# Twelve tiles' columns loaded from a second layout, three tiles projected by an uncentred W_in, and the first group's norm in two halves

## The reference

```python
def rmsnorm(x, g): return x * rsqrt(mean(x * x) + eps) * g
h = einsum('bld,ed->ble', rmsnorm(layernorm(x), g_res), W_in) + b_in
h_patch = rmsnorm(ctx, g_init)[..., :512]
# scan over the context rows, s[i] = a * s[i - 1] + u[i], with u and a from dt and h_patch
plug = clip(cumsum(boundary_mask) - 1, 0, 3201)     # boundaries from cumsum(mask)
x = x + s[plug] + h
x = x + gelu(layernorm(x) @ w1 + b1) @ w2 + b2      # 512 -> 2048 -> 512
```

## Time and profile before

| what | value |
|---|---|
| time, median of 3 runs | 837.85 us (837.53 to 838.92) |
| the profiled execution, its own time | 837.43 us |
| its span on the core | 835.7 us |
| PE busy | 826.4 us, 99% |
| DVE, ACT, POOL busy | 315.2, 294.5, 256.3 us |
| granted TensorE clock | 1.00 |

### The profile page before, as it was taken

The page is one execution under the profiler, slowest core; times in us unless marked ns, Lnnn a source line. Parts: engine busy times, 40 slices in busy tenths (PEclk is TensorE's granted clock), DMA queues, the critical chain, the costliest instruction groups (busy, mean ns, idle before and its releaser), DMA issues.

```text
span 835.7 us, 10792 instructions
## 1 busy us (share of the span) xinstructions
PE 826.4 (99%) x3770; PEld 680.8 (81%) x3770; DVE 315.2 (38%) x513; ACT 294.5 (35%) x542; POOL 256.3 (31%) x236
## 2 busy tenths in 40 slices
PE   8999999999999999999999999999999999999998
PEld 5887888788888888888888888888888888888886
DVE  6899661664241333233332423143113311242112
ACT  5667446432622253224422262222222322222221
POOL 2273538950533026301631062305300250001000
PEclk9999999999999999999999999999999999999999
DMA  9858984251226022601233113302300230010001
GB/s 239 256 169 276 259 264 179 88 148 27 76 88 174 0 75 77 169 15 66 72 110 89 50 48 113 50 0 102 51 0 1 89 62 0 0 51 0 1 1 50
DMA packets 37327, 74.95 MB, mean 90 GB/s; under 512 B 6176, under 2 KB 6176, under 8 KB 35536
## 3 DMA queue, kind: packets, MB, share of 16 engines
q1 hardware_dynamic: 28324, 62.81, 23.3%
q0 software_dynamic: 4608, 8.39, 6.3%
q10 hardware_dynamic: 4368, 3.42, 1.4%
HBM read 47.87 MB, written 22.84 MB: 85 GB/s over the span
## 4 chain that ended last, share of the span: by engine, by line
PE 85%; POOL 4%; DVE 4%; DMA 2%; issue 2%; SPq 1%; ACT 1%; ACTq 0%; DVEq 0%; POOLq 0%
PE acc L859 14%; PE acc L861 14%; PE acc L860 14%; PE h_bank L859 14%; PE h_bank L861 13%; PE h_bank L860 13%; DMA xa_odd<-in_x_dram 2%; PE t_bank L918 2%; POOL w_lo L525 1%; POOL x_cur L624 1%; POOL cl L544 1%; DVE h_lo L1040 1%; POOL w_lo L531 1%; DVE st_a L1035 1%; SPq L348 0%
## 5 line engine op out<-in xcount | busy, mean ns | idle before, releaser
L1265 DVE TENSOR_TENSOR h_lo<-g_f,h_hi 128x512 fp32r<-128x512 f32 x128 | 99.9, 781 | 430.3 <-ACT g_f L796 420.9
L794 ACT ACTIVATE h_hi<-h_bank,b_c 128x512 fp32r<-128x512 f32 x128 | 88.2, 689 | 430.6 <-PE h_bank L861 425.7
L859 PE MATMUL h_bank<-xt_hi,w_hi 128*128 128x512 f32 x512 | 199.9, 390 | 0.6 <-POOL w_lo L525 0.6
L859 PE MATMUL acc<-w_hi,h_hi 128*128 128x512 f32 x512 | 199.8, 390 | 0.0
L861 PE MATMUL h_bank<-xt_hi,w_lo 128*128 128x512 f32 x512 | 199.3, 389 | 0.0
L860 PE MATMUL h_bank<-xt_lo,w_hi 128*128 128x512 f32 x512 | 199.2, 389 | 0.0
L861 PE MATMUL acc<-w_hi,h_lo 128*128 128x512 f32 x512 | 199.2, 389 | 0.0
L860 PE MATMUL acc<-w_lo,h_hi 128*128 128x512 f32 x512 | 199.2, 389 | 0.0
L859 PEld LDWEIGHTS h_bank<-xt_hi,w_hi 128*128 128x128 f32 x512 | 96.1, 188 | 20.7 <-issue 1.0
L861 PEld LDWEIGHTS h_bank<-xt_hi,w_lo 128*128 128x128 f32 x512 | 96.1, 188 | 20.0
L861 PEld LDWEIGHTS acc<-w_hi,h_lo 128*128 128x128 f32 x512 | 96.1, 188 | 20.0
(11 more groups left out here) (164 smaller groups left out, 695.8 us busy)
## 6 DMA issues: line engine op xcount, KB each, us to landing
out_dram<-x_cur SPq DMA_DIRECT2D x32, 256.0 KB, 2.1
x_next<-x_part SPq DMA_DIRECT2D x7, 1024.0 KB, 5.1
...
```

The source lines that it names most:

```text
L794: act.activation(h_hi[:, m % HB, :], h_bank[m % 2][:], ACT.Gelu, bias=b1_c[:, m:m + 1])
L859: nc.tensor.matmul(dst, a_hi, b_hi, start=first, stop=False)
L1265: dve.tensor_tensor(h_lo[:, m % HB, :], g_f32[:], h_hi[:, m % HB, :].bitcast(F32), ALU.subtract).then_inc(h_split, 1)
```

## The change: what it does

It has three parts.

**Columns from a second layout.** A second copy of x, `x_cols`, lies in DRAM with each tile's columns already turned. For tiles 20 to 31 (`HOSTED`) SP loads 256 KB each of it, in 12 DMAs issued at t = 5 to 10, into quarters of `w_raw` that are still free. PE has no `transpose_first` for these tiles; `tile_high` and `tile_low` read SBUF where they read PSUM (`columns(t)`). The loads of the later quarters of w1 wait until those tiles have been read.

**Three tiles by a W_in that is not centred.** Tiles 0 to 2 (`RAW`) are multiplied by `first_hi` and `first_lo`, W_in times `g_res` without centring. What centring would have taken away is added back on DVE by `fix_tile` (one operation a tile, with `neg_sums` and POOL's `mean_ra`), before `tile_add`. The column sums come from three POOL additions (`add_w_in`), one fp32 matmul with `ones`, and one ACT copy. All four `win_lo` are made on DVE. Tile 3 takes its sums in `acc3`, tile 4 in `h_bank0`. `h_bank0` is also what `mask_totals` writes, which is moved to t = 6 and waits for `tile_add(4)`. The work of the mask is placed one tile later on DVE, `carry(0)` and `add_carry(0)` too, while `count_positions` and the second half of `one_hots_p` stay where they were. SP stores the second table block at t = 18, not 20. Tiles 7, 9 and 11 have their statistics on ACT. WARM, the number of dummy transposes at the start of PE's list, goes from 14 to 10.

**The norm in halves.** Statistics of rows 0 and 1 at t = 27; norm of 0 and 1, then the statistics of 2 and 3, at t = 29; norm of 2 and 3 at t = 30. POOL scales two rows, makes two low parts of w1, scales the other two, and makes two more.

```diff
-WARM = 14
+STORE0 = 17
+WARM = 10
+RAW = 3
...
-ON_ACT = (6, 8, 10, 18, 20, 21, 22, 23, 24, 25, 26, 27)
+ON_ACT = (6, 7, 8, 9, 10, 11, 18, 20, 21, 22, 23, 24, 25, 26, 27)
...
+HOSTED = tuple(range(20, NT))
...
+        def columns(t):
+
+            if t not in HOSTED:
+                return first_bank[t % 3][:]
+            u = t - HOSTED[0]
+            q = 1 + u // K
+            return w_raw[:, u % K, q * D:(q + 1) * D]
...
+        def sums_bank(t):
+
+            return {3: acc[3], 4: h_bank[0]}[t] if t in (3, 4) else p_bank[(t + 2 * (t < 3)) % 3]
...
-            for k in range(K):
+            for t, k in ((0, 0), (1, 3)):
+                sp.dma_start(xa(t), x_v[0, :, t, :]).then_inc(xa_loaded[t], 16)
                 sp.dma_start(win_raw[:, k, :], win_v[:, k, :]).then_inc(win_loaded[k], 16)
+            sp.dma_start(xa(2), x_v[0, :, 2, :]).then_inc(xa_loaded[2], 16)
...
+                if 5 <= t < 5 + len(HOSTED) // 2:
+                    for u in (2 * (t - 5), 2 * (t - 5) + 1):
+                        sp.dma_start(columns(HOSTED[u]), x_cols[HOSTED[u], :, :]).then_inc(cols_loaded[u], 16)
+                if t == STORE0:
                     store_block(0, cl)
-                if t == 20:
+                if t == STORE0 + 1:
...
+                    wait_apart(sp, x_lo, HOSTED[K])
...
+            wait_apart(sp, x_lo, HOSTED[2 * K])
             load_w1(2)
             load_w2(2)
+            wait_apart(sp, x_lo, NT)
...
+            def add_w_in(k):
+
+                pool.wait_ge(win_scaled, k + 1)
+                src = win_g[:, 0, :] if k == 1 else win_sum
+                ins = pool.tensor_tensor(win_sum, src, win_g[:, k, :], ALU.add)
+                if k < K - 1:
+                    step(ins)
...
+            def mean_scales(t0, n):
+
+                pool.wait_ge(ra_ready, t0 + n)
+                u = slice(t0, t0 + n)
+                pool.tensor_tensor(mean_ra[:, u], mv_a[:, u, 0], ra[:, u], ALU.mult).then_inc(mean_ra_ready, n)
+
+            add_w_in(1)
+            add_w_in(2)
+            add_w_in(3)
             scales(0, 2)
+            mean_scales(0, 2)
             scales(2, 2)
+            mean_scales(2, 1)
...
-            for k in range(K):
+            first_scale(slice(0, 2), rb_first)
+            for k in (0, 1):
                 low_w1(0, k, 1)
-            group_scale(0)
+            first_scale(slice(2, TI), rb_ready)
+            for k in (2, 3):
+                low_w1(0, k, 1)
...
+                if t in HOSTED:
+                    act.wait_ge(cols_loaded[t - HOSTED[0]], 16)
+                else:
+                    act.wait_ge(x_turned, t + 1)
...
-            for k in range(K):
-                act.activation(g_wide[:, k, :], ones[:], ACT.Copy, scale=g_res_c[:, k:k + 1]).then_inc(g_made, 1)
...
                 act.wait_ge(win_loaded[k], 16)
+                act.activation(first_hi[:, k, :], win_raw[:, k, :], ACT.Copy, scale=g_res_c[:, k:k + 1]).then_inc(first_hi_done, 1)
...
+            high_first(0)
             tile_high(0)
+            high_first(1)
+            scale_w_in(0)
+            scale_w_in(1)
+            tile_high(1)
+            high_first(2)
+            scale_w_in(2)
+            high_first(3)
+            scale_w_in(3)
+            tile_high(2)
+            act.wait_ge(win_summed, 1)
+            act.activation(neg_sums[:], acc[3][:], ACT.Copy, scale=-1.0).then_inc(neg_sums_made, 1)
             high_w_in(0)
-            tile_high(1)
-            high_w_in(1)
-            tile_high(2)
-            high_w_in(2)
-            high_w_in(3)
             tile_high(3)
+            for k in range(1, K):
+                high_w_in(k)
+            tile_high(4)
+            tile_high(5)
...
+            def sum_w_in():
+
+                pe.wait_ge(win_added, 1)
+                nc.tensor.matmul(acc[3][:], ones[:], win_sum, start=True, stop=True).then_inc(win_summed, 1)
...
+                if t == RAW:
+                    pe.wait_ge(neg_sums_made, 1)
+                if t >= 5:
+                    pe.wait_ge(acc_read, t - 4 if t < 8 else t - 2)
...
             warm_up()
-            sum_w_in(0)
-            sum_w_in(1)
             transpose_first(0)
-            sum_w_in(2)
-            sum_w_in(3)
+            project_raw(0, 0)
             transpose_first(1)
+            project_raw(0, 1)
+            project_raw(1, 0)
+            project_raw(1, 1)
+            project_raw(0, 2)
+            project_raw(1, 2)
             transpose_first(2)
-            for k in (0, 1):
-                project_first_part(0, k)
-                project_first_part(1, k)
-            project_first_part(2, 0)
-            project_first_part(2, 1)
+            project_raw(0, 3)
+            project_raw(1, 3)
+            sum_w_in()
             transpose_first(3)
-            for k in (2, 3):
-                for t in range(3):
-                    project_first_part(t, k)
+            for k in range(K):
+                project_raw(2, k)
             transpose_first(4)
             for t in range(3, NT):
-                if t + 2 < NT:
+                if t + 2 < HOSTED[0]:
                     transpose_first(t + 2)
-                if t == 4:
+                if t == 6:
+                    pe.wait_ge(acc_read, 5)
                     mask_totals()
-                if t == 15:
+                if t == 16:
                     pe.wait_ge(consts_made, 5)
                     carry(0, cl, acc[3][:])
                 if t == 16:
@@ -949,7 +1024,7 @@
                 if t == 19:
                     pe.wait_ge(block_ready, 1)
                     carry(1, cl_next, acc[3][:])
-                if t == 19:
+                if t == 20:
                     count_before()
...
+            fixed = []
+
+            def fix_tile(t):
+
+                dve.wait_ge(mean_ra_ready, t + 1)
+                ins = dve.scalar_tensor_tensor(x1(t), neg_sums[:], mean_ra[:, t:t + 1], xa(t), ALU.mult, ALU.add)
+                fixed.append(own.inc(ins))
...
+                if t < RAW:
+                    dve.wait_ge(dve_self, fixed[t])
+                rows = x1(t) if t < RAW else xa(t)
+                dve.scalar_tensor_tensor(x1(t), sums_bank(t)[:], ra[:, u:u + 1], rows, ALU.mult, ALU.add).then_inc(acc_read, 1)
...
-                if t == 1:
+                if t == 3:
                     mask_parts()
-                if t == 5:
+                if t == 6:
                     mask_positions()
-                if t == 6:
+                if t == 7:
                     mask_carries()
-                if t == 7:
...
                 if t == 15:
-                    add_carry(0, acc[3][:], cl, (0, 1))
                     scan_row(1, cl_next, 1)
                 if t == 16:
-                    add_carry(0, acc[3][:], cl, (2, 3))
+                    add_carry(0, acc[3][:], cl, (0, 1))
                     scan_row(1, cl_next, 2)
                     scan_row(1, cl_next, 3)
+                if t == 17:
+                    add_carry(0, acc[3][:], cl, (2, 3))
                 if t == 17:
                     count_rows()
                 if t == 18:
                     add_carry(1, acc[3][:], cl_next, (0, 1))
                     add_carry(1, acc[3][:], cl_next, (2, 3))
-                if t == 19:
+                if t == 20:
                     finish_plug()
-                for v in (t + LEAD,) if t < 22 else (2 * t - 18, 2 * t - 17) if t < 25 else ():
+                for v in {0: (), 1: (), 2: (4,), 3: (5,)}[t] if t < LEAD else (t + LEAD,) if t < 22 else (2 * t - 18, 2 * t - 17) if t < 25 else ():
                     if v in ON_DVE:
                         tile_stats(v)
-                if t in (27, 28):
-                    for i in (2 * (t - 27), 2 * (t - 27) + 1):
-                        second_stats(0, i)
+                if t == 27:
+                    second_stats(0, 0)
+                    second_stats(0, 1)
                 if t == 29:
-                    for i in range(TI):
-                        second_norm(0, i)
+                    second_norm(0, 0)
+                    second_norm(0, 1)
+                    second_stats(0, 2)
+                    second_stats(0, 3)
                 if t == 30:
                     transposed_low(0, 0)
                     transposed_low(0, 1)
+                    second_norm(0, 2)
+                    second_norm(0, 3)
                 if t == 31:
                     transposed_low(0, 2)
                     transposed_low(0, 3)
```

130 lines of the change are left out of this document (76 added, 54 removed).

## The result

| | before | with the change |
|---|---|---|
| median | 838.11 us (837.53 to 838.92, 6 runs) | 841.47 us (839.89 to 842.81, 6 runs) |
| ratio | | 1.004, 95% interval 1.0027 to 1.0052 |
| profiled execution | 837.43, span 835.7 | 842.81, span 840.7, granted clock 0.996 |

The change makes the kernel slower by 0.4%, 3.4 us. The profiled execution is the slowest of the six; the spans of three others lie 1.7 to 2.9 us under it, and these three had a granted clock of 0.998 in the mean, where it and the other two had 0.996.

The account below looks back on a forecast made before the run. PE, busy 99% of the span, was taken as the bound, with DVE second in the first layer. Terms -5.5 + 1.05 + 3.1 - 0.2 + 2.3 = +0.75 on 837.43 gave 838.2, forecast as median 838.4; range 834.0 to 841.3.

Parts of the forecast that it names:

- the head: Start to tile 6: PE's earlier start is spent waiting about 3.1 us for tile_add(4); tile 6 at 34.1, +1.05 us.
- costed at nothing: Column loads, table stores, w1's loads and the second layer: taken to add no time, 0 us.
- The middle: Tile 14 to carry(1): mask work a tile later on DVE makes PE wait, +3.1 us, bounds 0 and 5.
- Transposes gone: Tiles 20 to 31: PE saves 0.45 us of transposes and slower start per tile, -5.5 us.
- rival B: Head and tile 6: PE's clock falls in new idle times; 839.7 us, up to 842.2 with both; chance 0.27.
- The hand-over: End of the first layer: norms of rows 2 and 3 blocked beside POOL's w1 low parts, +2.3 us.
- rival A: Middle and hand-over: the gain survives, costing 0.5 and 0 there; 833.7 us; chance 0.29.

Follow-up runs that it names:

- fill_head: The whole change with 10 dummy transposes between tile 0's transposes and its first product; 839.55 us, ratio 1.0012.
- all_mended: The whole change with dummy transposes in the head and ahead of tile 6, ACT's squares behind tile 31's high part, and the norm whole; 836.69 us, ratio 0.9981.
- pool_waits: The whole change with POOL's last two low parts of w1's first quarter made only after the four norms; 838.90 us, ratio 1.001.
- cols_alone: The kernel before with only the columns of tiles 20 to 31 taken from the second layout; 837.66 us, ratio 0.9992.
- cols_squares: cols_alone with ACT's squares of context block 2 moved behind tile 31's high part; 838.79 us, ratio 1.0006.
- cols_best: cols_squares with the second table block stored at t = 19 instead of 20, count_before and finish_plug a tile later; 837.20 us, ratio 0.9991.
- cols_filled: cols_alone with 20 dummy transposes of PE ahead of the first norm transposes at t = 30; 836.24 us, ratio 0.999.

## Why the prediction was wrong

I forecast no change, 838.4, with a range up to 841.3; it is slower, 841.47. Three terms failed: the clock, which was in no term of the sum and cost 3.0 us (1.38 at tile 6 and 1.65 at tile 31); the head, put at 1.05 and measured at 3.19; and the first norms, costed at nothing and waited for 1.96 us, because ACT stood before the load `cl`. The middle was put 2.3 us too high and hid part of this. By its steps:

- **Transposes gone, -5.5**: right. The rows of tiles 21 to 28 are 2.72 us apart in the changed kernel (87.87 to 90.59).
- **The head, +1.05**: the mechanism was right (DVE's queue behind the column sums, a wait of 3.1 foreseen and 3.2 measured at `tile_add(4)`), the size was not: 3.19. Everything is 2.1 us later than I put it. The first slice of W_in came only at 6.19, the first product at 8.36 for 7.9, and the products behind it start 0.43 us apart until about 12, as where the granted clock is 0.50, so the sums ended at 18.0 for 16.4. (The column of the granted clock reads 1.00 from 8 to 12 us; the cold start does not show in it.) The first centring starts at 18.78 and DVE's row ends at 33.3, 14.5 us for the 13.9 of the sum. The prediction's own terms do not give its 34.1: 1.36, 0.7 and 0.3 behind 31.0 to 31.3 are 33.4 to 33.7, a head of 0.3 to 0.6 (PE's row adds up to 22.6, not 22.8). That the true stretch was 2.9 us (33.3 to 36.24) made the 34.1 better than its sum. fill_head gives 1.2 of the lateness back. This is the first half of rival B, which I had set apart from the likeliest case.
- **The middle, +3.1**: over-sized, one wait of 0.8 us at `carry(1)`; the waits for `h_lo` (0.15 and 0.65) are part of the head. DVE was busy for 44.15 of the 50 us from 30 to 80, 88% and not the over 95% that I gave as a sign; before, it was 45.95. A later PE is held up less by DVE: in all_mended, where PE comes to tile 7 about 2.8 us sooner, waits for one-hots and `h_lo` come up. With the 1.2 us of fill_head alone they do not.
- **The hand-over, +2.3**: right for the norms of rows 2 and 3, 1.8 (1.3 + 1.0 foreseen, 1.05 + 0.75 measured), and for the reason, which pool_waits shows. What the Trainium skill says of the shared interface (SBUF — State Buffer, section Who interferes with whom) holds in kind for a 128x512 fp32 norm: 2.35 us for two beside POOL, 1.00 alone.
- **Costed at nothing**: this step failed too. "The stores of the table and w1's loads keep their distance" looked at loads that the change adds or delays. It did not ask which loads have their own time while the tiles get shorter. `cl` (9.6 us from issue to use before, only 0.43 waited for) and the gather were the next bound, and nothing in the earlier trace rows shows them, because they are waits of ACT and DVE. With the store at t = 19 or 20 and the columns, the statistics of row 3 wait for the gather until 107.5 to 109.4 (cols_alone, cols_squares, cols_best, cols_filled). In the changed kernel, whose store is already at t = 18, it is the load alone: 1.96 us.
- **The clock**: rival B had a chance of 0.27 and its second half held: 1.38 at tile 6, 1.65 at tile 31, where it foresaw no fall. I had priced one fall at up to 2.5. Both its halves came, which the range left out; that its 842.2 lies near the result is in part luck, as it had the middle at 3.1 and the first norms at nothing. Its bound, that the clock falls from idle times of about 2.5 us on, did not hold: it fell behind 1.9 us in pool_waits and not behind 3.4 in cols_squares. It belongs in the sum as soon as a forecast itself puts 3 us of idle time on PE.

With head 3.2, clock 3.0, hand-over 3.8 and middle 0.8, against -5.5, the result is +5.3 for the profiled execution, and 3.4 in the median, where not every execution has both falls of the clock: three of six have 0.998 instead of 0.996. Of rival A the middle held (0.5 foreseen, 0.8 measured) and the hand-over did not. Its number, 833.7, is near what the columns alone reach once their chain is moved too (833.39), by chance.
